# An attention and expert layer on one core: score chunks, rotation and maxima chunks in another order, and the first two sequences loaded, written and prepared by need

## The chip, the cores and the metric

One core of one Trainium2 chip runs the whole layer in one launch. The metric is the device time of that launch in microseconds, the median of several runs. The notes use these names: PE (TensorE), DVE (VectorE), ACT (ScalarE), POOL (GpSimd), SP (SyncE, which here only issues DMAs).

## What is computed

16 sequences of 256 tokens, width 128, go through causal attention with 16 heads of 8 and rotary position tables, a residual and a layer norm, then a layer of 8 experts of which each token takes one (its largest gate, with a capacity of 512 tokens an expert), a residual and a second layer norm.

```python
q = (x @ wq + bq); k = (x @ wk + bk); v = (x @ wv + bv)      # 16 heads of 8
q = _apply_rope(q, cos, sin); k = _apply_rope(k, cos, sin)
scores = jnp.einsum('bhqd,bhkd->bhqk', q, k) / jnp.sqrt(jnp.float32(HEAD_DIM)) + causal
attn = jax.nn.softmax(scores, axis=-1)
x = _layernorm(x + (attn @ v) @ wo + bo)
probs = softmax(x @ wg); idx = argmax(probs); mask = one_hot(idx)
locations = cumsum(mask) - mask; mask = mask * (locations < C)
x = _layernorm(x + gate * (W[idx] @ x + b[idx]))
```

## The kernel before

Every engine has its instruction stream written out by hand, with semaphores between them. The work is software-pipelined over the sequences. In step s the kernel works on sequence n = s + 2 (its transposes, its q and k projections, the rotation), a = s + 1 (its parts are written to DRAM and loaded back in another layout), b = s (row maxima of the scores, the v projection), c = s - 1 (scores again with the maximum subtracted, exp, product with v), d = s - 2 (division, output projection, first norm, gate, experts) and e = s - 3 (second norm, output). Steps run from -2 to 17. A step has 14 slots, and each engine's program lists what it does in slot 0, 1, 2 and so on. Within a slot the order is that of the code.

The scores of a sequence are cut into 11 chunks (`CHUNKS`): eight of two groups of heads, two of four, one of eight. In slot k + 2 PE makes chunk k of the scores of c in ps_b (line 820, "ps_b chunk"), ACT takes its exp (line 473), and in slot k + 3 PE multiplies it with v into ps_pv (line 853, "PV chunk k"). The maxima chunks are scores in ps_a (line 830), whose row maxima DVE takes (line 631). `maxima_at` places them: chunks 2 to 10 of b in slots 0 to 8, and chunks 0 and 1 of a in slots 12 and 13. ps_a and ps_b each have two banks, so chunk k waits for the reader of chunk k - 2.

```python
if slot < NCH - EARLY:
    return (b, slot + EARLY) if has(b) else (None, 0)
if slot >= SLOTS - EARLY:
    return (a, slot - (SLOTS - EARLY)) if has(a) else (None, 0)
```

When all row maxima of b are there, DVE widens them to heads and splits them into three bf16 parts in max_parts (lines 674 to 687), PE turns them (line 840, slot 11), ACT copies them to max_rows (line 495) and issues two DMAs that put them into q_plain (line 502), which the ps_b chunks of the next step read. After that ACT makes rot_1 (line 512) and then the exp of chunk 10.

The experts come in two blocks, one for each half of the tokens (`experts(d, n, 0)` in slot 12, `experts(d, n, 1)` in slot 13, lines 774 to 794). Both write ps_m, so the second waits until DVE has selected from the first (line 616). The gate (lines 692 to 709) and the capacity test (lines 713 to 725) are on DVE in slots 9 and 10, followed by the rotation's four products (lines 730, 733) and their addition (line 739). ACT splits off the first bf16 part (line 512) and POOL the other two (lines 424 to 430). SP writes the three parts in 12 DMAs (line 314), and once they have landed it loads k_plain and q_diag of a, the maxima operands (lines 326, 329), and then q_plain and k_diag of b, the operands of ps_b (lines 337, 340).

At the end of a step ACT copies the sums out of ps_pv (slot 13), and at the start of the next the weighted values (slot 0). DVE takes the reciprocals of the sums in slots 1 and 2 (line 640).

At the start SP loads the tables and weights, DVE clears v_diag, swaps and splits the weights, PE turns the biases (line 753), and only then come the first transposes (line 880) and projections (lines 774 to 776). In step -2 `start_late` prepares the expert weights (lines 560, 562, 764) and the bf16 tables (lines 566 to 570) behind the rotation of sequence 0. ACT writes the head marks into k_diag (`mark_heads`, line 448) in slot 6 of steps -1 and 0.

## Time and profile before

| | |
|---|---|
| median of 3 runs | 492.28 us (491.29 to 495.66) |
| the profiled execution's own time | 493.83 us |
| its span, first to last instruction | 492.2 us |
| mean granted TensorE clock | 0.948 |
| busy: PE, DVE, ACT, POOL | 418.6, 345.4, 169.0, 165.2 us |
| moved by DMA | 47.29 MB, mean 96 GB/s |

Busy time counts instructions from start to end. PE's matmuls overlap each other and their ends are modelled, so idle time in front of a matmul is shown a little short.

### The profile page before, as it was taken

What the parts mean: (1) busy time and instruction counts of PE and PEld (TensorE: products, weight loads), DVE (VectorE), ACT (ScalarE), POOL (GpSimd) and SP (SyncE); (2) the same over time, 40 slices, a digit from 0 to 9 for tenths busy, and PEclk for the clock granted to TensorE, in tenths of its full rate; (3) what the DMA queues carried; (4) which work ended last, traced back from release to release, by engine and by line L of the source; (5) the groups of instructions that cost most, each with busy time, mean ns of one, the idle gap of its engine ahead of it and who ended that gap; (6) DMA issues with size and microseconds to landing.
All of it is one profiled execution on the core that took longest, in us unless ns stands there. A gap on an engine that the chain in (4) does not pass through costs nothing.

```text
span 492.2 us, 10410 instructions
## 1 busy us (share of the span) xinstructions
PE 418.6 (85%) x3270; PEld 362.4 (74%) x3270; DVE 345.4 (70%) x910; ACT 169.0 (34%) x370; POOL 165.2 (34%) x288
## 2 busy tenths in 40 slices
PE   2527398999999999999999999999999999989551
PEld 2425287979788888888888878787879787868441
DVE  7677346678787877788787878778777786844542
ACT  4404134333342424243333434333434342424100
POOL 5423202131424242433424251525252523231232
PEclk9997588999999999999999999999999999999856
DMA  4163977939385856777585849393939393310000
GB/s 119 48 102 90 150 137 107 140 87 137 74 147 86 144 79 135 91 126 97 121 104 121 106 105 126 90 135 82 149 83 140 84 141 65 30 31 1 11 1 21
DMA packets 145443, 47.29 MB, mean 96 GB/s; under 512 B 104317, under 2 KB 141697, under 8 KB 145418
## 3 DMA queue, kind: packets, MB, share of 16 engines
q1 hardware_dynamic: 141194, 43.30, 55.0%
q10 hardware_dynamic: 3456, 1.57, 1.8%
q0 software_dynamic: 768, 2.10, 1.5%
q8 instruction: 13, 0.21, 0.2%
q14 instruction: 12, 0.10, 0.1%
HBM read 30.70 MB, written 14.68 MB: 92 GB/s over the span
## 4 chain that ended last, share of the span: by engine, by line
PE 65%; DVE 17%; issue 6%; ACT 5%; SPq 2%; DMA 2%; POOL 1%; ACTq 1%; DVEq 0%; POOLq 0%
PE ps_pv L853 27%; PE ps_m L774 6%; PE ps_b L820 5%; PE ps_m L775 5%; PE ps_m L776 5%; DVE y_sel L616 4%; PE ps_a L830 4%; PE ps_m L794 3%; PE ps_b L805 2%; ACT probs L473 2%; PE ps_a L805 2%; PE ps_n L861 2%; DMA k_diag<-plain_parts 1%; SPq L314 1%; PE ps_n L901 1%
## 5 line engine op out<-in xcount | busy, mean ns | idle before, releaser
L853 PE MATMUL ps_pv<-probs,v_diag 128*128 128x64 f32 (+3 forms) x1024 | 191.1, 322 | 6.1 <-ACT probs L473 6.1
L853 PEld LDWEIGHTS ps_pv<-probs,v_diag 128*128 128x128 f32 x1024 | 150.3, 193 | 16.1 <-ACT probs L473 9.1
L473 ACT ACTIVATE probs<-ps_b 128x512 f32<-128x512 f32 (+1 forms) x176 | 96.9, 559 | 141.3 <-PE ps_b L805 140.5
L631 DVE TENSOR_REDUCE row_max<-ps_a 128x2 f32<-128x512 f32 (+3 forms) x176 | 109.8, 634 | 36.7 <-PE ps_a L805 36.4
L830 PE MATMUL ps_a<-k_plain,q_diag 128*128 128x64 bf16 (+3 forms) x512 | 66.3, 242 | 12.9 <-DMA q_diag<-plain_parts 7.2
L820 PE MATMUL ps_b<-q_plain,k_diag 128*128 128x64 bf16 (+3 forms) x512 | 65.9, 237 | 2.1 <-DMA k_diag<-plain_parts 2.1
L616 DVE TENSOR_REDUCE y_sel<-ps_m 128x128 f32<-128x1024 f32 x32 | 39.2, 1225 | 38.0 <-PE ps_m L794 37.3
L830 PEld LDWEIGHTS ps_a<-k_plain,q_diag 128*128 128x128 bf16 x512 | 35.3, 102 | 23.4 <-DVE row_max L631 13.0
L820 PEld LDWEIGHTS ps_b<-q_plain,k_diag 128*128 128x128 bf16 x512 | 37.6, 99 | 10.2 <-DMA k_diag<-plain_parts 2.4
L413 POOL COPY v_diag<-v_rows 64x128 f32<-64x128 f32 x64 | 18.6, 291 | 78.2 <-ACT v_rows L487 76.2
L805 PE MATMUL ps_a<-mask_a_bf,ident_bf 128*128 128x128 bf16 (+2 forms) x176 | 44.6, 253 | 0.0
L424 POOL TENSOR_TENSOR rot_rest<-rot 128x512 f32<-128x512 f32 x16 | 18.6, 1159 | 76.7 <-ACT rot L512 63.0
L805 PE MATMUL ps_b<-mask_b_bf,ident_bf 128*128 128x128 bf16 (+2 forms) x176 | 43.4, 247 | 0.0
L350 POOL TENSOR_SCALAR rs<-mv 128x2 f32<-128x2 f32 x32 | 7.4, 230 | 100.6 <-DVE mv L601 100.6
L455 ACT ACTIVATE sums<-ps_pv 64x256 f32<-64x256 f32 x16 | 6.1, 381 | 83.0 <-PE ps_pv L853 83.0
L774 PE MATMUL ps_m<-we_hi,x1t_hi 128*128 128x512 f32 x64 | 29.7, 464 | 4.1 <-DVE y_sel L616 4.1
L640 DVE RECIPROCAL inv_den<-sums 128x128 f32<-128x128 f32 x32 | 29.8, 938 | 2.6 <-ACT sums L456 2.6
L774 PE MATMUL ps_m<-xt_hi,w_hi 128*128 128x256 f32 x64 | 21.2, 331 | 10.6 <-DVE xt_lo L669 10.6
L361 POOL TENSOR_SCALAR y_out<-z,mv,rs 128x128 f32<-128x128 f32 x32 | 25.5, 801 | 3.6 <-POOL rs L352 3.6
L775 PE MATMUL ps_m<-we_lo,x1t_hi 128*128 128x512 f32 x64 | 26.2, 410 | 0.0
L776 PE MATMUL ps_m<-we_hi,x1t_lo 128*128 128x512 f32 x64 | 26.1, 408 | 0.0
L794 PE MATMUL ps_m<-route_rows,route 128*128 128x512 f32 x64 | 26.0, 406 | 0.0
(141 smaller groups left out, 695.9 us busy)
## 6 DMA issues: line engine op xcount, KB each, us to landing
plain_parts<-rot SPq DMA_DIRECT2D x192, 64.0 KB, 2.0
k_plain<-plain_parts SPq DMA_DIRECT2D x16, 384.0 KB, 3.8
q_diag<-plain_parts SPq DMA_DIRECT2D x32, 192.0 KB, 5.4
q_plain<-plain_parts SPq DMA_DIRECT2D x16, 384.0 KB, 6.1
k_diag<-plain_parts SPq DMA_DIRECT2D x32, 192.0 KB, 6.5
x_in<-in_L_attn_x_dram SPq DMA_DIRECT2D x16, 128.0 KB, 5.7
x_res<-in_L_attn_x_dram SPq DMA_DIRECT2D x16, 128.0 KB, 3.1
out_dram<-y_out POOLq DMA_DIRECT2D x16, 128.0 KB, 2.5
```

The lines of the kernel that those rows point to most:

```text
L473: act.activation(probs[:, k % PR, 0:cols], ps_b[k % 2][:, 0:cols], ACT.Exp, scale=SCALE)\
L616: dve.tensor_reduce(y_sel[:, t, :], ps_m[:, :, :].rearrange("p a (e f) -> p f (a e)", e=4), AX.X, ALU.max).then_inc(s_["moe_taken"], 1)
L631: last = dve.tensor_reduce(row_max[:, NBLK - 1 - j, groups[0]:groups[-1] + 1], scores[:, :, col:col + width(j)], AX.X, ALU.max)
L640: dve.reciprocal(inv_den[:, half_cols], sums[:, half_cols]).then_inc(s_["den_done"], 1)
L774: pe.matmul(out, sh, mh, start=start, stop=False, skip_group_check=True)
L775: pe.matmul(out, sh, ml, start=False, stop=False, skip_group_check=True)
L776: return pe.matmul(out, sl, mh, start=False, stop=stop, skip_group_check=True)
L794: mm = pe.matmul(ps_m[:, h, :], route[:, tok], route_rows[:, 512 * h:512 * h + 512], start=False, stop=True, skip_group_check=True)
L805: return pe.matmul(v, ident_bf[:, :], rows, start=False, stop=True, skip_group_check=True)
L820: pe.matmul(ps_b[k % 2][:, col:col + width(j)], diag_block(k_diag[q], g, j), q_plain[q][:, g, BLK * j:S], start=(i == 0), stop=False, skip ...
L830: pe.matmul(ps_a[k % 2][:, col:col + width(j)], diag_block(q_diag[at], g, NBLK - 1 - j), k_plain[at][:, g, 0:width(j)], start=(i == 0), st ...
L853: mm = pe.matmul(ps_pv[:, g // 4, BLK * j:S], v_diag[q][:, j, 128 * g:128 * g + 128], probs[:, k % PR, col:col + width(j)], start=(j == 0 ...
```

## The change

1. Order on PE. Maxima chunks of b move to slots 0, 2, 3, 4, 5, 6, 7 and two in slot 8 (`MAXIMA_IN`). The turned maxima come behind the PV chunk of slot 11, and the second expert block behind the last PV chunk.
2. DVE. The second selection moves to slot 3 of the next step, the rotation's products ahead of the capacity test, and the first half of the reciprocals to slot 13 of the step before.
3. POOL takes over the widening and splitting of the maxima and the addition of the rotation. ACT copies sums and weighted values together in slot 13.
4. The start. Loads are split and ordered (identity, x, wq, bq, wk, bk, then wv and the rest, then the tables), each with its own semaphore. The turning of the biases moves behind the first transposes. `start_late` moves from step -2 to step -1. ACT makes the bf16 tables. For sequences 0 and 1, ACT issues the six writes of rot_1, and SP loads the ps_b operands directly behind the maxima operands.

```diff
+MAXIMA_IN = {0: (2,), 2: (3,), 3: (4,), 4: (5,), 5: (6,), 6: (7,), 7: (8,), 8: (9, 10)}
...
-            if slot < NCH - EARLY:
-                return (b, slot + EARLY) if has(b) else (None, 0)
             if slot >= SLOTS - EARLY:
-                return (a, slot - (SLOTS - EARLY)) if has(a) else (None, 0)
-            return None, 0
+                return [(a, slot - (SLOTS - EARLY))] if has(a) else []
+            return [(b, k) for k in MAXIMA_IN.get(slot, ())] if has(b) else []
...
-                    write(rot_1, 0, "rot1_done")
+                    if not (is_step(s, -1) or is_step(s, 0)):
+                        write(rot_1, 0, "rot1_done")
...
+                    if is_step(s, -1) or is_step(s, 0):
+                        sp.wait_ge(s_["start_pool"], 2 + 2 * a)
+                        load_b(a, q)
...
+                    after(pool, "a_taken", b, NCH, NCH)
+                    after(pool, "ex_ready", b)
+                    pool.tensor_tensor(max_wide[:, :, :].rearrange("p i (g h) -> p (i g) h", g=PAIRS),
...
+                    pool.tensor_copy(max_part(0), by_half(max_wide)).then_inc(s_["parted"], 1)
...
+                    after(pool, "roped", n, 1, 1)
+                    pool.tensor_tensor(rot[:, :, :], rot_c[:, :, :], rot_s[:, :, :], ALU.add).then_inc(s_["rot_done"], 1)
...
+            def write_part_1(n):
+
+                after(act, "rot1_done", n, 1, 1)
+                act.nop(nofuse=True)
+                for qk, taus in ((0, Q_PARTS[0]), (1, K_PARTS[0])):
+                    for tau in taus:
+                        act.dma_start(of_seq(plain, n)[qk, :, :, tau].rearrange("h d g x -> (h d) (g x)"),
+                                      rot_1[:, qk, :]).then_inc(s_["parts_written"], 16)
...
+                    if slot == 8 and is_step(s, -2):
+                        narrow_tables()
+                    if slot == 8 and is_step(s, -1):
+                        write_part_1(0)
+                        mark_heads(0)
+                    if slot == 12 and is_step(s, -1):
+                        write_part_1(1)
+                        mark_heads(1)
...
-                    if slot in (12, 13) and has(d):
-                        select(d, slot - 12)
-                    if slot in (1, 2) and has(d):
-                        after(dve, "sums_copied", d, 1, 1)
-                        half_cols = slice(128 * (slot - 1), 128 * slot)
-                        dve.reciprocal(inv_den[:, half_cols], sums[:, half_cols]).then_inc(s_["den_done"], 1)
+                    if slot == 12 and has(d):
+                        select(d, 0)
+                    if slot == 3 and has(e):
+                        select(e, 1)
+                    if slot == 13 and has(c):
+                        after(dve, "sums_copied", c, 1, 1)
+                        dve.reciprocal(inv_den[:, 0:128], sums[:, 0:128]).then_inc(s_["den_done"], 1)
+                    if slot == 0 and has(d):
+                        dve.reciprocal(inv_den[:, 128:S], sums[:, 128:S]).then_inc(s_["den_done"], 1)
...
-                    if slot == 10 and is_step(s, -2):
+                    if slot == 10 and is_step(s, -1):
                         start_late()
```

On PE, slots 11 to 13 of a step in the middle. ps_a and ps_b are the maxima and score chunks, ps_pv the PV chunks, `we_hi` with `x1t_hi` the experts. Before, from PV chunk 9 on:

```order
L853 MATMUL ps_pv<-probs,v_diag 128x128 [waits exp_done]
...
L830 MATMUL ps_a<-k_plain,q_diag 128x256 [waits a_taken]
...
L774 MATMUL ps_m<-we_hi,x1t_hi 128x512 [waits moe_taken]
...
L794 MATMUL ps_m<-route_rows,route 128x512
L853 MATMUL ps_pv<-probs,v_diag 128x64 [waits exp_done]
L853 MATMUL ps_pv<-probs,v_diag 128x64 x7
```

The changed kernel at the same place:

```order
L881 MATMUL ps_pv<-probs,v_diag 128x128 [waits exp_done]
...
L869 MATMUL ps_a<-k_plain,q_diag 128x256 [waits a_taken]
...
L881 MATMUL ps_pv<-probs,v_diag 128x64 [waits exp_done]
L881 MATMUL ps_pv<-probs,v_diag 128x64 x7
L814 MATMUL ps_m<-we_hi,x1t_hi 128x512 [waits moe_taken]
...
L834 MATMUL ps_m<-route_rows,route 128x512
```

The expert block that waits for the selection (`moe_taken`) has changed places with the last PV chunk.

On DVE, slots 9 to 13 of such a step. Before:

```order
L687 TENSOR_TENSOR max_parts<-max_rest,max_parts 128x4x2x8
L692 TENSOR_REDUCE logits<-ps_n 128x16
...
L719 SCALAR_TENSOR_TENSOR kept<-ps_n,chosen_f 128x16
...
L730 SCALAR_TENSOR_TENSOR rot_cs<-ps_m,bias_cols,cst 128x256
...
L739 TENSOR_TENSOR rot<-rot_cs 128x512
L631 TENSOR_REDUCE row_max<-ps_a 128x2
L616 TENSOR_REDUCE y_sel<-ps_m 128x128
L631 TENSOR_REDUCE row_max<-ps_a 128x2
L616 TENSOR_REDUCE y_sel<-ps_m 128x128
```

Now:

```order
L727 TENSOR_REDUCE logits<-ps_n 128x16 [waits logits_ready]
...
L753 SCALAR_TENSOR_TENSOR rot_cs<-ps_m,bias_cols,cst 128x256 [waits rot_done,qk_ready]
...
L768 SCALAR_TENSOR_TENSOR kept<-ps_n,chosen_f 128x16
...
L682 TENSOR_REDUCE row_max<-ps_a 128x2 [waits widened,a_ready]
L668 TENSOR_REDUCE y_sel<-ps_m 128x128 [waits moe_ready]
L682 TENSOR_REDUCE row_max<-ps_a 128x2 [waits a_ready]
L692 RECIPROCAL inv_den<-sums 128x128 [waits sums_copied]
```

The operations on the maxima and the addition are gone from DVE, the products stand ahead of the test `kept`, and a reciprocal stands where the second selection was.

On SP, the writes and loads of sequences 0 and 1 (the parts are plain_parts). Before:

```order
L314 DMA plain_parts<-rot 16x8x256 x12
L326 DMA k_plain<-plain_parts 96x2048
L329 DMA q_diag<-plain_parts 48x32x64 x2
L303 DMA x_in<-in_L_attn_x_dram 128x2x128
L314 DMA plain_parts<-rot 16x8x256 x12
L326 DMA k_plain<-plain_parts 96x2048
L329 DMA q_diag<-plain_parts 48x32x64 x2
L337 DMA q_plain<-plain_parts 96x2048
L340 DMA k_diag<-plain_parts 48x32x64 x2
```

Now, for sequence 0:

```order
L323 DMA plain_parts<-rot 16x8x256 [waits rot2_done]
L323 DMA plain_parts<-rot 16x8x256 x3
L323 DMA plain_parts<-rot 16x8x256 [waits rot3_done]
L323 DMA plain_parts<-rot 16x8x256
L336 DMA k_plain<-plain_parts 96x2048 [waits parts_written,start_pool]
L339 DMA q_diag<-plain_parts 48x32x64 x2
L302 DMA q_plain<-plain_parts 96x2048 [waits start_pool]
L305 DMA k_diag<-plain_parts 48x32x64 x2
```

Sequence 0's q_plain and k_diag stood behind all writes and maxima operands of sequence 1; now they follow their own maxima operands.

## Rows read from the trace of the kernel before

**Rows 1.** The page, part 1: busy time, share of the span, instructions.

```profile
PE 418.6 (85%) x3270; PEld 362.4 (74%) x3270; DVE 345.4 (70%) x910; ACT 169.0 (34%) x370; POOL 165.2 (34%) x288
```

**Rows 2.** ACT's timeline, one middle step: start, us, line, out<-in [idle before].

```profile
212.42 1.09 ACT L473 ACTIVATE probs<-ps_b 128x512 f32<-128x512 f32 x2
...
228.26 1.61 ACTq L502 DMA_DIRECT2D q_plain<-max_rows  x2
...
230.65 0.60 ACT L473 ACTIVATE probs<-ps_b 128x512 f32<-128x512 f32 x1
236.44 0.38 ACT L455 ACTIVATE sums<-ps_pv 64x256 f32<-64x256 f32 x1 [5.19 <-PE ps_pv L853]
...
238.03 0.60 ACT L473 ACTIVATE probs<-ps_b 128x512 f32<-128x512 f32 x1
```

**Rows 3.** PE's timeline in the same step: start, us, line, out<-in.

```profile
212.63 0.22 PE L805 MATMUL ps_a<-mask_a_bf,ident_bf 128*128 128x128 bf16 x1
213.07 1.13 PE L853 MATMUL ps_pv<-probs,v_diag 128*128 128x256 f32 x4 [0.22 <-ACT probs L473]
...
214.25 0.22 PE L805 MATMUL ps_b<-mask_b_bf,ident_bf 128*128 128x128 bf16 x1
214.31 0.33 PE L830 MATMUL ps_a<-k_plain,q_diag 128*128 128x192 bf16 x2
...
225.05 0.40 PE L820 MATMUL ps_b<-q_plain,k_diag 128*128 128x128 bf16 x4
...
227.24 0.22 PE L840 MATMUL ps_n<-stacked_bf,max_parts 128*128 128x64 bf16 x2 [0.40 <-DVE kept L719]
...
232.56 0.50 PE L774 MATMUL ps_m<-we_hi,x1t_hi 128*128 128x512 f32 x1 [0.15 <-DVE y_sel L616]
...
234.51 1.89 PE L853 MATMUL ps_pv<-probs,v_diag 128*128 128x64 f32 x16
...
237.47 0.34 PE L830 MATMUL ps_a<-k_plain,q_diag 128*128 128x192 bf16 x2 [0.24 <-DVE row_max L631]
```

**Rows 4.** Groups by line: busy us, mean ns of one | idle before it.

```profile
L616 DVE TENSOR_REDUCE y_sel<-ps_m 128x128 f32<-128x1024 f32 x32 | 39.2, 1225 | 38.0 <-PE ps_m L794 37.3
...
L424 POOL TENSOR_TENSOR rot_rest<-rot 128x512 f32<-128x512 f32 x16 | 18.6, 1159 | 76.7 <-ACT rot L512 63.0 <-issue 13.7
...
L739 DVE TENSOR_TENSOR rot<-rot_cs 128x512 f32<-128x512 f32 x16 | 11.1, 692 | 1.0
...
L687 DVE TENSOR_TENSOR max_parts<-max_rest,max_parts 128x64 bf16<-128x64 f32 x16 | 3.6, 225 | 0.6
```

**Rows 5.** DVE's timeline, the widening product in step 0 and in a middle step.

```profile
46.00 0.22 DVE L674 TENSOR_TENSOR max_wide<-row_max,cst 128x64 f32<-128x64 f32 x1
...
222.90 0.35 DVE L674 TENSOR_TENSOR max_wide<-row_max,cst 128x64 f32<-128x64 f32 x1
```

**Rows 6.** Timeline of the start, of SP, PE and DVE.

```profile
28.19 0.34 SPq L326 DMA_DIRECT2D k_plain<-plain_parts  x1
...
31.51 0.58 PE L774 MATMUL ps_m<-xt_hi,w_hi 128*128 128x256 f32 x1 [8.49 <-DVE xt_lo L669]
...
36.78 3.25 DVE L631 TENSOR_REDUCE row_max<-ps_a 128x2 f32<-128x512 f32 x5
...
37.61 8.01 SPq L314 DMA_DIRECT2D plain_parts<-rot  x12
...
54.52 0.61 PE L830 MATMUL ps_a<-k_plain,q_diag 128*128 128x256 bf16 x2 [6.62 <-DMA q_diag<-plain_parts]
...
59.40 0.61 PE L820 MATMUL ps_b<-q_plain,k_diag 128*128 128x256 bf16 x2 [2.07 <-DMA k_diag<-plain_parts]
```

**Rows 7.** The chain of waits, at the start and at the end: start, us, what.

```profile
8.60 2.30 PE ps_n L753 x10
...
47.12 0.33 SPq L326
...
459.54 1.74 PE ps_pv L853 x16
```

More of the change, by code:

```diff
@@ L474, in step @@
                             .then_inc(s_["exp_done"], 1)
-                    if slot == 0 and has(d):
-                        copy_pairs(weighted, 0).then_inc(s_["pv_copied"], 1)
                     if slot == 7 and has(d):
@@ L621, in step @@
                 for slot in range(SLOTS):
-                    t, k = maxima_at(slot, a, b)
-                    if t is not None:
+                    for t, k in maxima_at(slot, a, b):
                         after(dve, "a_ready", t, NCH, k + 1)
@@ L646, in step @@
                         dve.tensor_tensor(attn[:, :], weighted[:, :], inv_den[:, :], ALU.mult).then_inc(s_["normed"], 1)
-                    if slot == 3 and has(e):
+                    if slot == 4 and has(e):
                         add_experts(e)
@@ L710, in step @@
                                           ALU.is_equal).then_inc(s_["chosen_done"], 1)
+                    if slot == 9 and is_step(s, -2):
+                        split_wv()
+                    if slot == 10 and has(n):
+                        after(dve, "qk_ready", n, 1, 1)
+                        after(dve, "rot_done", n)
+                        for i in range(2):
+                            dve.scalar_tensor_tensor(out=rot_c[:, i, :], in0=ps_m[:, 0, S * i:S * i + S],
+                                                     scalar=bias_cols[:, 2 * i:2 * i + 1], in1=C("cos"),
+                                                     op0=ALU.add, op1=ALU.mult)
+                            last = dve.scalar_tensor_tensor(out=rot_s[:, i, :], in0=ps_m[:, 1, S * i:S * i + S],
+                                                            scalar=bias_cols[:, 2 * i + 1:2 * i + 2], in1=C("sin"),
+                                                            op0=ALU.add, op1=ALU.mult)
+                        last.then_inc(s_["roped"], 1)
                     if slot == 10 and has(d):
@@ L822, in step @@
                         masks(ps_b[k % 2], CHUNKS[k], mask_b_bf, False).then_inc(s_["b_ready"], 1)
-                    t, k = maxima_at(slot, a, b)
-                    if t is not None:
+                    for t, k in maxima_at(slot, a, b):
                         at = p if t is b else q
@@ L832, in step @@
                         masks(ps_a[k % 2], CHUNKS[k], mask_a_bf, True).then_inc(s_["a_ready"], 1)
-                    if slot == 13 and has(d):
-                        experts(d, n, 1)
-                    if slot == 11 and has(b):
-                        after(pe, "parted", b, 4, 4)
-                        if has(d):
-                            after(pe, "route_done", d, 1, 1)
-                        for i in range(NBLK // 2):
-                            mm = pe.matmul(ps_n[:, BLK * i:BLK * i + BLK],
-                                           max_parts[:, 2 * i:2 * i + 2, :].rearrange("p i m -> p (i m)"), stacked_bf[:, :],
-                                           start=(i == 0), stop=True, skip_group_check=True)
-                        mm.then_inc(s_["ex_ready"], 1)
                     if slot == 12 and has(d):
@@ L856, in step @@
                         mm.then_inc(s_["pv_ready"], 1)
+                    if slot == 11 and has(b):
+                        after(pe, "parted", b, 4, 4)
+                        if has(d):
+                            after(pe, "route_done", d, 1, 1)
+                        for i in range(NBLK // 2):
+                            mm = pe.matmul(ps_n[:, BLK * i:BLK * i + BLK],
+                                           max_parts[:, 2 * i:2 * i + 2, :].rearrange("p i m -> p (i m)"), stacked_bf[:, :],
+                                           start=(i == 0), stop=True, skip_group_check=True)
+                        mm.then_inc(s_["ex_ready"], 1)
+                    if slot == 13 and has(d):
+                        experts(d, n, 1)
                     if slot == 4 and has(d):
```

150 lines of the change are left out of this document (77 added, 73 removed).

## The prediction

> **What bounds the kernel now.** I read the page first, then the timelines of one middle step engine by engine, then the start and the chain of waits at the end. The reader is to see that TensorE is the bound: busy for 418.6 of 492.2 us [rows 1]. In the middle the steps repeat: exp 0 of a sequence starts at 212.42 and the next sequence's at 238.03, a step of 25.61 us [rows 2]. Of it PE stands still at four places [rows 3]: before PV chunk 0 (213.07, waits for exp 0), before a maxima chunk (237.47, waits for a row maximum), before the transposed maxima (227.24, wait for the capacity test on DVE) and before the second expert block (232.56, waits for the selection of the first). The idle shown is 0.22 + 0.24 + 0.40 + 0.15 = 1.01 us, but it counts only from the modelled end of the last matmul. A mask matmul that is followed at once has its successor 0.06 us after its own start (214.25, 214.31), and the one at 212.63 waits 0.44 us for its successor: issue really stopped for 0.38 us, 0.16 more than shown. So the four are 0.38 + 0.40 + 0.56 + 0.32 = 1.66 us, and 23.95 us of a step are work of PE. That is what the middle can give.
>
> The start is another matter: the first exp waits for PE's first ps_b matmul at 59.40, which waits for k_diag of sequence 0 [rows 6]. Those operands stand in SP's queue behind the writes and loads of sequence 1. The end is a serial chain of some 31 us after the last PV chunk, which ends at 461.3 [rows 7].
>
> **The start, edit by edit.** (a) The cover at the very beginning stays: DVE's memset of v_diag ends at 5.96 in either kernel and its swaps and splits run to about 10.5. The ten bias matmuls take 2.30 us from 8.60 [rows 7]; the transposes, xt_hi and xt_lo no longer stand behind them but ahead, so the projections of sequence 0 begin at 10.9, not 12.85: 1.95 us less. The rotation's addition goes to POOL: 1.16 us by the subtraction of the same shape there against 0.69 on DVE [rows 4]. rot_1 of sequence 0 is done at 17.4 (18.9 before).
> (b) Sequence 1's projections began at 31.51 [rows 6] behind the expert weights and DVE's narrowing copies. Now they need only xt_lo, after rot_1 on ACT: 18.3. ACT then issues six writes and marks the heads. At SP's pace (12 writes in 8.01 us, [rows 6]) six writes are 4.0 us, and the marking takes 4.2, so ACT is free at 26; POOL, with its memsets in between, ends the rotation's addition of sequence 1 at about 27.5. rot_1 of sequence 1 is done at 28.1, against 37.5.
> (c) SP issues only six writes for sequence 0, from POOL's rot_2 (19.4) on, to 23.5. The loads began 1.5 us after the last write's issue ended (45.62 to 47.12, [rows 6, 7]), so they begin at 25.2, not 28.19. Sequence 1's maxima operands were usable 7.4 us after the load's issue and sequence 0's k_diag behind them 12.3 us after it (47.12 to 54.52 and 59.40). Now both sets of sequence 0 go in a row: 32.6 and 37.5. The former wait of the first exp, k_diag, is gone by 22 us; what is late next?
> (d) The eleven row maxima of sequence 0 start at 33 instead of 36.78 [rows 6] and take 9 us as before, to 42. Then POOL splits them (2.4 us, below), PE turns them, ACT copies (0.6), issues two DMAs (2.3 there) and they land 2 us later: 49.7. Sequence 1: its writes queue behind the loads of sequence 0 (37.5), land at about 39.2, its loads are usable at 46.6, and three maxima chunks stand ahead of ps_b: 49.2. Both agree: ps_b at 49.7 instead of 59.40, the term is **-9.7 us**. If the three sets of loads slow each other it is -6; with no such delay and a shorter chain, -12.
>
> **The step in the middle.** Count from the end of PV chunk 10. (1) Four copies on ACT, 1.59 us (236.44 to 238.03, [rows 2]), then exp 0, 0.60. PE's cover was five chunks of scores; now it is the second expert block, 1.95 us (232.56 to 234.51, [rows 3]), and five groups of about 0.27: 3.3 us. exp 0 ends at 3.30. The stall of 0.38 shrinks to under 0.1. (2) The selection of the first block (1.23, [rows 4]) runs under PV 10 (1.74): 0.32 gone. (3) DVE loses the five widening operations (0.22 to 0.32 each, 1.5 us with gaps) and the addition (0.69), and the second selection sits behind row maximum 4, so maxima chunks find their buffers free within 0.1: 0.40 shrinks to 0.1. At the tight places, the pair of chunks in slot 8 and xt_lo, 0.1 to 0.4 us are in hand when the row maxima are laid out one behind another at 0.46 to 0.62 each. (4) The turned maxima stand behind PV 8 (0.99 us later), but the capacity test now stands behind the rotation products (1.65 us). From PV 0 (213.07), the projections are issued by 225.05 [rows 3] and done at +12.1, the products at +13.8, the test at +14.6; PE gets there at 227.24 - 0.56 + 0.99, +14.6. 0.56 shrinks to 0.1. (5) What is next: from the turned maxima ACT copies, issues DMAs for 1.61 us, copies rot_1, runs exp 10, which ends at 231.25, 4.0 us after 227.24 [rows 2, 3]. PE's work between is now also 4.0 us, because the expert block is behind PV 10: no slack, 0 to 0.1. (6) POOL's chain: last row maximum at 13.4 on this count, v_diag copies to 14.3, then five small operations. Such an operation has no row on POOL. Its ends are DVE's 0.22 for the same shape and POOL's 1.16 for 128x512 [rows 4]; I take 0.4, nearer the first, since it has an eighth of the columns, with gaps 2.1 in all: ready at 16.4, needed at 18.2. At the upper end 5.8 us would cost 1.9 a step, 27 in all. The addition on POOL ends some 2 us before ACT can take it, behind its DMA issues.
> Left over 0.15, so the step is **24.1 us, -1.5**. If the tight places add up, -0.9; if nothing is left, -1.66. SP's writes and loads start some 2 us later in a step, where the maxima operands have about 5 us in hand.
>
> A place where the trace and the notes speak against the change: the widening product on DVE took 0.22 us at 46.00 with POOL idle and 0.35 at 222.90 beside POOL's copies [rows 5]. The Trainium skill, SBUF — State Buffer, section "Who interferes with whom", says that a DVE instruction with two SBUF inputs and a GpSimd instruction that reads SBUF hold a shared port and the later one waits for the whole of the other. The trace agrees in kind, with 0.13 us. By that rule DVE's four router operations of this sort would each wait up to 0.4 us beside POOL's new chain, 1.6 us against 1.5 in hand: 0.1 a step, 1.4 in all.
>
> **The sum**, against the profiled execution (493.83 us; span 492.2 and 1.6 around it): start -9.7. The step with sequence 0's PV has no experts to cover ACT's chain, +0.8. The next -1.3, since the row maxima bound its start less. Eleven steps at -1.5: -16.5. Two steps near the end, with 2.2 us of stalls each, -1.9 each: -3.8. The last PV step: PV 0 waited 1.7 and the selection 0.6, and its second expert block (1.95) now runs behind the last PV chunk (459.54 to 461.3) under the copies and reciprocals; the late selection delays z1, which waits for nothing else there, by 0.55: -3.7. Together -34.2: 459.6. The median of the runs is 1.55 below the profiled execution, so I predict 458.
>
> **Rivals.** A: the stalls of the middle only change place (maxima pair, exp 10): -0.3 a step. Speaks for it that three places have under 0.15 us in hand; against it that DVE has 2.2 us less to do in a step. Then 16 us less gain: 474. B: the start gives only 3 us, since sequence 0's second set and sequence 1's first came together once before, between 47.12 and 59.40 [rows 6, 7], and now more of them lie close, and ACT's issues delay rot_1. Against it that most loads now start earlier, one after another. Then 465. C, slower: POOL's five small operations. If each took 1.5 us (7.5 with no gap, against the 4.0 us between 14.3 and 18.3), the turned maxima would come 3.5 us late in each of 14 steps, +49 over the sum: 507. It decides from 1.3 us an operation, where 2.4 us a step eats all the gain. For it: nothing but that the shapes are split in halves and POOL has no row for them. Against it: 1.16 us for eight times the columns. D: the addition on POOL holds rot_1 on ACT and so exp 10 (the change does not do what it says): it would have to be over 2 us later than I have it; at 1 us beyond, +14: 472.
>
> **How the numbers follow.** Forecast (start -6 to -12, step -1.2 to -1.66) 0.70; A 0.10; B 0.12; C 0.02; D 0.04; 0.02 for no change by several of them. The forecast's own ends are 452 and 466. To hold 8 in 10, B and part of A have to be in: 451 to 470. A change of 1% (5 us) is about what a measurement of this kernel can tell from none. Only C and the remainder reach that: faster 0.96, same 0.02, slower 0.02.
>
> **What would show it.** First ps_b matmul at about 50 us, ended by the maxima rows' DMA or by q_diag of sequence 1, not k_diag. exp 0 to exp 0 24.1 us. PE idle in a middle step under 0.3 us shown, with nothing before the second expert block. POOL's five small operations under 0.5 us each and done before PE asks. The second expert block of the last step behind the last PV chunk. I am wrong if the first ps_b is after 54, if a step is above 24.8, or if PE waits for max_parts or for exp 10 by more than 0.3 us in each step.

## The result, and the profile after

The changed kernel takes **461.94 us** (median of 4 runs, 461.80 to 464.61) against 491.78 us for the kernel before in the same comparison (4 runs, 489.36 to 495.66). The ratio is 0.940, 95% interval 0.933 to 0.947. Predicted were 458.0 us and a range of 451 to 470.

The page of the profiled execution (461.80 us, span 460.1), parts 1 and 2; the second part is in 40 slices of the span:

```profile
PE 410.3 (89%) x3270; PEld 359.2 (78%) x3270; DVE 317.8 (69%) x809; ACT 170.4 (37%) x375; POOL 207.8 (45%) x384
...
PE   3548598999999999999999999999999999999651
...
PEclk9999798999999999999999999999999999999957
```

PE is still the bound, with the same 3270 matmuls. DVE has 101 instructions fewer and POOL 96 more [rows 1].

The steps. ACT's timeline, the first exp of a sequence each time: the very first; sequences 2 and 13, which enclose eleven steps in the middle; and the two ends of the middle step that is read below:

```profile
53.81 0.60 ACT L517 ACTIVATE probs<-ps_b 128x512 f32<-128x512 f32 x1 [3.20 <-PE ps_b L845]
...
102.86 0.60 ACT L517 ACTIVATE probs<-ps_b 128x512 f32<-128x512 f32 x1 [1.01 <-PE ps_b L845]
...
199.82 0.60 ACT L517 ACTIVATE probs<-ps_b 128x512 f32<-128x512 f32 x1 [0.99 <-PE ps_b L845]
...
224.12 1.15 ACT L517 ACTIVATE probs<-ps_b 128x512 f32<-128x512 f32 x2 [0.99 <-PE ps_b L845]
...
369.28 0.60 ACT L517 ACTIVATE probs<-ps_b 128x512 f32<-128x512 f32 x1 [0.91 <-PE ps_b L845]
```

(369.28 - 102.86) / 11 = 24.22 us a step, where the kernel before has 25.61 [rows 2]. The stalls are gone. PE's timeline of that step, in order: turned maxima, last PV chunk, second expert block, the maxima chunk of slot 0 and the first PV chunk of the next sequence. All but the last PV chunk are the places of [rows 3]:

```profile
215.48 0.22 PE L890 MATMUL ps_n<-stacked_bf,max_parts 128*128 128x64 bf16 x2
...
219.53 2.00 PE L881 MATMUL ps_pv<-probs,v_diag 128*128 128x64 f32 x16
221.34 0.48 PE L814 MATMUL ps_m<-we_hi,x1t_hi 128*128 128x512 f32 x1
...
224.51 0.34 PE L869 MATMUL ps_a<-k_plain,q_diag 128*128 128x192 bf16 x2
...
224.77 1.13 PE L881 MATMUL ps_pv<-probs,v_diag 128*128 128x256 f32 x4
```

None of these lines shows an idle time (in brackets, it would be the wait in front of the instruction). Over the step, PE's idle time adds up to 0.11 us against 1.01. POOL's timeline of the same step shows its new chain, and DVE's the one place where it costs something:

```profile
211.75 0.29 POOL L424 TENSOR_TENSOR max_wide<-row_max,cst 128x64 f32<-128x64 f32 x1 [0.25 <-POOL v_diag L419]
212.18 0.24 POOL L431 CAST max_parts<-max_wide 128x64 bf16<-128x64 f32 x1
212.50 0.31 POOL L433 TENSOR_TENSOR max_rest<-max_wide,max_parts 128x64 f32<-128x64 f32 x1
212.94 0.24 POOL L437 CAST max_parts<-max_rest 128x64 bf16<-128x64 f32 x1
213.26 0.30 POOL L439 TENSOR_TENSOR max_parts<-max_rest,max_parts 128x64 bf16<-128x64 f32 x1
...
214.90 1.28 POOL L448 TENSOR_TENSOR rot<-rot_cs 128x512 f32<-128x512 f32 x1 [0.16 <-POOL seen L444]
```

```profile
215.57 0.63 DVE L774 TENSOR_TENSOR gate_kept<-n_kept,gate 128x2 f32<-128x2 f32 x1
```

The five operations end at 213.56, 1.9 us before PE asks.

The start is where the time fell short. PE's timeline there, the waits alone, then ACT's:

```profile
32.21 0.58 PE L869 MATMUL ps_a<-k_plain,q_diag 128*128 128x256 bf16 x2 [4.44 <-DMA q_diag<-plain_parts]
...
43.91 0.58 PE L814 MATMUL ps_m<-xt_hi,w_hi 128*128 128x256 f32 x1 [1.11 <-DVE xt_lo L722]
...
46.65 0.33 PE L890 MATMUL ps_n<-stacked_bf,max_parts 128*128 128x64 bf16 x2
...
53.08 0.59 PE L860 MATMUL ps_b<-q_plain,k_diag 128*128 128x256 bf16 x2 [3.43 <-DMA q_plain<-max_rows]
```

```profile
47.60 2.28 ACTq L550 DMA_DIRECT2D q_plain<-max_rows  x2
```

The first exp starts 6.3 us earlier than before (53.81; it was at 60.15), and what it waits for is no longer k_diag [rows 6] but the two DMAs of max_rows, whose issue ended at 49.88 and which landed at 53.08. (A landing is read here from the start of the first ps_b matmul that waited for it.)

By spans, 492.2 to 460.1: start -6.3, the step of the first PV +0.7 (24.14), the next -1.4 (24.91), eleven steps -15.4, the two behind them -4.4 (22.48 and 21.67), from the last exp 0 to the end -5.2 (46.67). Together -32.1; predicted were -34.2.

### The profile page after: what moved, and what is told of

The parts are those of the page before. It is cut to its first block and busy times, and to the rows that moved or that the text cites. A ratio compares the mean times of both kernels' runs of the same rounds, so it can differ in the third digit from the quotient of the medians.

```text
span 460.1 us, 10441 instructions
## 1 busy us (share of the span) xinstructions
PE 410.3 (89%) x3270; PEld 359.2 (78%) x3270; DVE 317.8 (69%) x809; ACT 170.4 (37%) x375; POOL 207.8 (45%) x384
## 5 line engine op out<-in xcount | busy, mean ns | idle before, releaser
L881 PEld LDWEIGHTS ps_pv<-probs,v_diag 128*128 128x128 f32 x1024 | 148.0, 192 | 12.0 <-ACT probs L517 6.2
L682 DVE TENSOR_REDUCE row_max<-ps_a 128x2 f32<-128x512 f32 (+3 forms) x176 | 108.3, 631 | 22.3 <-PE ps_a L845 21.9
L419 POOL COPY v_diag<-v_rows 64x128 f32<-64x128 f32 x64 | 18.4, 288 | 68.6 <-PE ps_pv L881 33.9
L860 PEld LDWEIGHTS ps_b<-q_plain,k_diag 128*128 128x128 bf16 x512 | 36.3, 98 | 11.5 <-issue 4.2
L692 DVE RECIPROCAL inv_den<-sums 128x128 f32<-128x128 f32 x16 | 15.2, 953 | 37.0 <-ACT sums L483 37.0
L814 PE MATMUL ps_m<-we_hi,x1t_hi 128*128 128x512 f32 x64 | 28.6, 448 | 1.3 <-DVE y_sel L668 1.3
L753 DVE SCALAR_TENSOR_TENSOR rot_cs<-ps_m,bias_cols,cst 128x256 f32<-128x256 f32 x32 | 15.3, 479 | 19.5 <-PE ps_m L816 19.5
L448 POOL TENSOR_TENSOR rot<-rot_cs 128x512 f32<-128x512 f32 x16 | 20.6, 1288 | 14.2 <-DVE rot_cs L756 12.5
```

The costliest lines, as they stand in the source:

```text
L682: last = dve.tensor_reduce(row_max[:, NBLK - 1 - j, groups[0]:groups[-1] + 1], scores[:, :, col:col + width(j)], AX.X, ALU.max)
L814: pe.matmul(out, sh, mh, start=start, stop=False, skip_group_check=True)
L860: pe.matmul(ps_b[k % 2][:, col:col + width(j)], diag_block(k_diag[q], g, j), q_plain[q][:, g, BLK * j:S], start=(i == 0), stop=False, skip ...
L881: mm = pe.matmul(ps_pv[:, g // 4, BLK * j:S], v_diag[q][:, j, 128 * g:128 * g + 128], probs[:, k % PR, col:col + width(j)], start=(j == 0 ...
```

## The experiments

Each is an edit of the changed kernel. A step is the mean of the same eleven as above; in the changed kernel and the six runs that alter only its start it is 24.20 to 24.23, so a tenth of a microsecond there is a difference. Where no interval is given, the time is that of one execution. The first exp comes at 53.4 to 55.5 us in the changed kernel and the six runs that alter its middle, so 1 us there tells nothing by itself.

**start_alone**: all orders of PE and DVE, POOL's share and ACT's copies as in the kernel before; the start as changed.

```diff
-MAXIMA_IN = {0: (2,), 2: (3,), 3: (4,), 4: (5,), 5: (6,), 6: (7,), 7: (8,), 8: (9, 10)}
+MAXIMA_IN = {i: (i + 2,) for i in range(9)}
...
-                    if slot == 12 and has(d):
-                        experts(d, n, 0)
+                    if slot in (12, 13) and has(d):
+                        experts(d, n, slot - 12)
...
```

> The changed kernel with its whole middle undone (orders on PE and DVE, POOL's share, ACT's copies), so only the start of the change is left. Theory T (start and middle are independent, the middle's gain is made of stalls of PE in each step): first exp at 53.8 us as in the changed kernel, a step in the middle back at 25.6, last exp 0 to the end 51.9, about 486 us, ratio 0.987. Rival R (part of the middle's gain comes from the later transfers and loads of the start, or the start's gain is given back in the first full steps): time outside 483 to 489, or a step away from 25.6 by over 0.2 us.

Measured: ratio 0.984 (0.9805 to 0.9876), median 482.66 us; the profiled execution, its longest, 487.16. First exp at 54.10, step (384.90 - 102.84) / 11 = 25.64, PE's idle in a middle step the same 1.01 us at the same four places as [rows 3], last exp 0 to the end 52.0. By the step, the first exp and the end, T holds: start and middle are independent. The median lies 0.3 us below the 483 at which R's range begins, the profiled execution fits T's 486. The start is worth 1.6% of the kernel, the middle and end the other 4.4.

Next, one part of the middle undone at a time.

**dve_splits**: widening, splitting and addition back on DVE, in slots 9 and 10.

```diff
-                    after(pool, "a_taken", b, NCH, NCH)
...
-                    pool.tensor_tensor(rot[:, :, :], rot_c[:, :, :], rot_s[:, :, :], ALU.add).then_inc(s_["rot_done"], 1)
...
+                        after(dve, "a_taken", b, NCH, NCH)
...
+                        dve.tensor_tensor(rot[:, :, :], rot_c[:, :, :], rot_s[:, :, :], ALU.add).then_inc(s_["rot_done"], 1)
```

> The changed kernel with widening and splitting of the maxima and the addition of the rotation back on DVE, all orders as changed. Theory T (DVE has room: some 22 of 24.2 us busy; the orders on PE removed the stalls, and POOL's part only took DVE's work off): the step stays within 24.2 to 24.6, total 462 to 467. Rival P (the offload is what buys the middle, since DVE's row maxima would again be late): the step goes to 25.0 or more, with PE idle before maxima chunks or before the turned maxima by over 0.6 us a step, total over 472.

**expert_ahead**: second expert block ahead of the last PV chunk, second selection in slot 13.

```diff
-                    if slot == 12 and has(d):
-                        select(d, 0)
-                    if slot == 3 and has(e):
-                        select(e, 1)
+                    if slot in (12, 13) and has(d):
+                        select(d, slot - 12)
...
-                    if slot == 12 and has(d):
-                        experts(d, n, 0)
+                    if slot in (12, 13) and has(d):
+                        experts(d, n, slot - 12)
...
```

> The changed kernel with the second expert block back ahead of the last PV chunk and the second selection back in slot 13. Theory T (stalls of their own places): the waits before the second expert block (0.3) and before PV chunk 0 (0.4) come back, the step is 24.8 to 24.9, and the tail from the last exp 0 grows by about 2 us: total about 472. Rival A (the stalls only change place): the step stays below 24.4.

**maxima_even**: the maxima chunks one to a slot.

```diff
-MAXIMA_IN = {0: (2,), 2: (3,), 3: (4,), 4: (5,), 5: (6,), 6: (7,), 7: (8,), 8: (9, 10)}
+MAXIMA_IN = {i: (i + 2,) for i in range(9)}
```

> The changed kernel with the maxima chunks one to a slot again, chunks 2 to 10 in slots 0 to 8. Theory T: the wait before the maxima chunk of slot 0 or 1 comes back in part (0.1 to 0.4 us a step): step 24.3 to 24.6, total 463 to 468. Rival N (the places of the maxima chunks do not matter now that DVE is relieved): step 24.2 within 0.05, total within 1 us of 462.

**test_ahead**: on DVE the block of the capacity test stands ahead of the block of the rotation's products, both in slot 10.

```diff
+                    if slot == 10 and has(d):
+                        after(dve, "egate_done", d, 1, 1)
...
                     if slot == 10 and has(n):
...
-                    if slot == 10 and has(d):
-                        after(dve, "egate_done", d, 1, 1)
...
```

> The changed kernel with the capacity test on DVE ahead of the rotation's products again. Theory T (each edit keeps DVE's queue just in time for PE; the products may be a little later, since rot_1 waited for ACT and not for POOL in the changed kernel, 1.85 us): step 24.2 to 24.5, the wait before the turned maxima (0.07) gone, total 462 to 466. Rival D (POOL's addition then comes too late for rot_1 and exp 10, or DVE stands behind the location matmuls): step 24.8 or more, with PE waiting before PV chunk 10, ps_b chunk 10 or the next experts.

**turned_ahead**: the turned maxima ahead of the PV chunk of slot 11.

```diff
+                    if slot == 11 and has(b):
+                        after(pe, "parted", b, 4, 4)
...
                     k = slot - PV_SLOT
...
-                    if slot == 11 and has(b):
-                        after(pe, "parted", b, 4, 4)
```

> The changed kernel with the turned maxima ahead of PV chunk 8 again. Theory T (the capacity test on DVE ends just when PE arrives, 0.07 us late, so whatever PE does before it is cover): PE waits some 1.0 us there in every step, step 25.1 to 25.3, total 474 to 478. Rival A (the stall is made good by the slack that exp 10 gains): PE waits, but the step stays below 24.6.

| | time, us | step, us | over the changed kernel's 24.22 |
|---|---|---|---|
| dve_splits | 478.39 | 25.30 | +1.08 |
| expert_ahead | 485.20 | 25.57 | +1.35 |
| maxima_even | 476.05 | 25.27 | +1.05 |
| test_ahead | 468.24 | 24.72 | +0.50 |
| turned_ahead | 471.76 | 25.11 | +0.89 |
| the whole middle (start_alone) | 482.66 | 25.64 | +1.42 |

Undone alone, the five cost 4.87 us a step; the whole middle undone costs 1.42. (start_alone also puts back the reciprocals, ACT's copy of the weighted values and the addition of the experts' output, which no run undoes alone.) PE's timelines of one middle step each say where. dve_splits:

```profile
248.08 0.22 PE L892 MATMUL ps_n<-stacked_bf,max_parts 128*128 128x64 bf16 x2 [1.11 <-DVE kept L770]
```

expert_ahead, the maxima chunk of slot 0 and the second expert block:

```profile
233.37 0.34 PE L866 MATMUL ps_a<-k_plain,q_diag 128*128 128x192 bf16 x2 [1.30 <-DVE row_max L682]
...
252.65 0.49 PE L811 MATMUL ps_m<-we_hi,x1t_hi 128*128 128x512 f32 x1 [0.15 <-DVE y_sel L668]
```

maxima_even, the chunks of slots 0 and 1:

```profile
231.03 0.34 PE L869 MATMUL ps_a<-k_plain,q_diag 128*128 128x192 bf16 x2 [0.24 <-DVE row_max L682]
...
232.43 0.34 PE L869 MATMUL ps_a<-k_plain,q_diag 128*128 128x192 bf16 x2 [0.74 <-DVE row_max L682]
```

test_ahead, the first expert block, and turned_ahead, the turned maxima:

```profile
220.63 0.49 PE L814 MATMUL ps_m<-we_hi,x1t_hi 128*128 128x512 f32 x1 [0.64 <-DVE rot_cs L771]
```

```profile
218.50 0.22 PE L879 MATMUL ps_n<-stacked_bf,max_parts 128*128 128x64 bf16 x2 [0.97 <-DVE kept L768]
```

Every one of these waits ends with DVE, although it is far from full: 19.65 of 25.27 us busy in dve_splits, 18.86 of 25.53 in expert_ahead. What counts is not its busy share but what stands in its queue in front of the instruction that PE waits for. DVE's timeline in expert_ahead, just before PE's wait, shows how:

```profile
231.82 0.95 DVE L690 RECIPROCAL inv_den<-sums 128x128 f32<-128x128 f32 x1 [1.31 <-ACT sums L483]
232.69 0.63 DVE L682 TENSOR_REDUCE row_max<-ps_a 128x2 f32<-128x512 f32 x1
```

The reciprocal of slot 13 waits 1.31 us for ACT's copy of the sums and takes 0.95, and the row maximum for which PE waits stands behind it. In the changed kernel PE spends those microseconds in the second expert block. In the kernel before this wait was absent too, because the reciprocals stood in slots 1 and 2. So the early reciprocal needs the late expert block, and the free slot 1 of `MAXIMA_IN` is room for the second reciprocal, which maxima_even fills. This is read from DVE's timeline; no run undoes such a pair together. By the expectations: P holds for dve_splits, and T is wrong. For expert_ahead A is wrong (the stall comes back) and so is T, by a factor of two (25.57, not 24.9). For maxima_even both are wrong, since 25.27 is 0.7 above the top of T's range. For test_ahead, 24.72 lies between T's 24.5 and D's 24.8; the wait is one of those that D names: the expert block needs ps_m, which the rotation's products read. turned_ahead came as T said (25.11 a step), with a total 2 us under T's range.

Then the start.

**start_by_sp**: sequences 0 and 1 written by SP alone, their ps_b operands loaded in their own steps.

```diff
-                    if not (is_step(s, -1) or is_step(s, 0)):
-                        write(rot_1, 0, "rot1_done")
+                    write(rot_1, 0, "rot1_done")
...
-                    if is_step(s, -1) or is_step(s, 0):
-                        sp.wait_ge(s_["start_pool"], 2 + 2 * a)
-                        load_b(a, q)
-                if has(b) and not (is_step(s, 0) or is_step(s, 1)):
+                if has(b):
+                    if is_step(s, 0) or is_step(s, 1):
+                        sp.wait_ge(s_["start_pool"], 2 + 2 * b)
...
-                        write_part_1(0)
...
-                        write_part_1(1)
```

> The changed kernel, but sequences 0 and 1 written by SP alone (no writes from ACT) and their ps_b operands loaded in their own steps, behind the next sequence's writes and loads, as before. Everything else of the start stays as changed. Theory L (the order of writes and loads is the larger part of the start's 6.3 us): first exp at 57 to 59, since k_diag of sequence 0 again stands behind sequence 1's set. Rival C (compute order is what brought the gain: projections of sequence 1 at 18.4 instead of 31.5): first exp below 55.5, and SP's transfers early enough anyway.

Measured 462.04 us, first exp at 52.96: not later than in the changed kernel. L is wrong, C holds. Once the projections come early, k_diag of sequence 0 is there in time in the old order too, and no gain of writes and loads "by need" shows. (The total hides 1.5 us: the end takes 48.21 us here, for which see the last steps below.)

**late_early**: `start_late` of DVE and PE in step -2 again.

```diff
-                    if slot == 10 and is_step(s, -1):
+                    if slot == 10 and is_step(s, -2):
                         start_late()
...
```

> The changed kernel with the expert weights' preparation (DVE and PE) back in step -2, ahead of sequence 1's transposes. Theory L: sequence 1 is written some 10 us later, but the chain of sequence 0 does not need it, so the first ps_b moves only by what the third maxima chunk of sequence 1 adds: first exp at 55 to 58. Rival C: the first exp goes back by over 5 us, to 59 or more.

Measured 466.12 us, first exp at 58.34, 4.5 us later: between the two expectations, and outside the scatter. PE's timeline:

```profile
30.13 0.58 PE L814 MATMUL ps_m<-xt_hi,w_hi 128*128 128x256 f32 x1 [8.93 <-DVE xt_lo L722]
...
57.61 0.59 PE L860 MATMUL ps_b<-q_plain,k_diag 128*128 128x256 bf16 x2 [3.36 <-DMA q_plain<-max_rows]
```

Neither sequence 1's chunks (the third at 53.54) nor its own data hold ps_b, but again max_rows: issued until 52.47, landed 5.1 us later, behind sequence 1's loads, which SP issued from 45.26 to 50.82.

**b1_in_step_1** and **short_chain** ask whether that landing depends on the bytes in flight or on when the chain ends. The first, timed again as b1_repeated:

```diff
-                    if is_step(s, -1) or is_step(s, 0):
+                    if is_step(s, -1):
                         sp.wait_ge(s_["start_pool"], 2 + 2 * a)
                         load_b(a, q)
-                if has(b) and not (is_step(s, 0) or is_step(s, 1)):
+                if has(b) and not is_step(s, 0):
+                    if is_step(s, 1):
+                        sp.wait_ge(s_["start_pool"], 2 + 2 * b)
```

> The changed kernel, only sequence 1's q_plain and k_diag are loaded in step 1 and not behind its maxima operands. Theory Q (the two DMAs of max_rows landed 3.2 us after their issue and not 2.0, because these 0.75 MB were moving): they land within 2.2 us, the first exp is 1 us earlier, at 52.8. Rival K (the landing time is that of the DMAs themselves, or another set takes that place): within 0.3 us of 53.8.

short_chain, where besides the lines shown DVE widens and splits for sequence 0, behind its last row maximum:

```diff
-                    if slot == 11 and has(b):
+                    if slot == (9 if is_step(s, 0) else 11) and has(b):
                         after(pe, "parted", b, 4, 4)
```

> The changed kernel, for sequence 0 alone: DVE widens and splits the maxima (some 1.0 us instead of POOL's 1.8), and PE turns them ahead of the projections of sequence 2, not behind them (46.65). Theory E (the chain row maxima, split, turn, ACT, DMA sets the first exp): turned at 44.5, first exp at 51.7 to 52.3, total 1.5 to 2.1 us less than 461.9. Rival S (sequence 1's operands and its third maxima chunk, at 49.2, are as late): first exp above 53.3.

The repetition of the first:

> The kernel of b1_in_step_1 again, timed in rounds, since one execution gave 456.77 us. Theory Q: the gain over the changed kernel (461.9) is 4 to 5 us and holds over executions: median 456 to 458, ratio 0.925 to 0.935. Rival V (that execution was one of the short ones): median 460 or more, ratio 0.935 to 0.94.

b1_in_step_1 took 456.77 us, first exp 51.18; the repetition 458.92 (457.80 to 459.78, 6 runs), ratio 0.932 (0.928 to 0.937), first exp 52.17. short_chain took 460.98, first exp 53.80. The waits of ps_b and the issue of max_rows, in b1_repeated:

```profile
47.62 2.28 ACTq L552 DMA_DIRECT2D q_plain<-max_rows  x2
```

```profile
51.45 0.58 PE L862 MATMUL ps_b<-q_plain,k_diag 128*128 128x256 bf16 x2 [1.78 <-DMA q_plain<-max_rows]
```

and in short_chain:

```profile
45.02 2.28 ACTq L551 DMA_DIRECT2D q_plain<-max_rows  x2
```

```profile
53.07 0.59 PE L881 MATMUL ps_b<-q_plain,k_diag 128*128 128x256 bf16 x2 [2.35 <-DMA q_plain<-max_rows]
```

b1_repeated against the changed kernel is the clean pair: with sequence 1's 0.75 MB out of the way, the DMAs issued at the same moment (47.62 and 47.60) land 1.6 us after their issue's end, not 3.2. (The 128 KB load of x_in, which stands behind them in SP's queue, went out 2.8 us earlier with it.) short_chain is less clean. Its DMAs were issued 2.6 us earlier and landed at 53.07 instead of 53.08, but SP's loads of sequence 1 also went out 1.4 us later, first the changed kernel's, then its own:

```profile
40.25 0.33 SPq L336 DMA_DIRECT2D k_plain<-plain_parts  x1
```

```profile
41.70 0.32 SPq L336 DMA_DIRECT2D k_plain<-plain_parts  x1
```

So the landing moved with the loads; what the earlier issue alone would have gained stays open. Q holds for b1_in_step_1 and E is wrong. S has the time right but not the cause: ps_b waited for max_rows. K is wrong on the time, but right that another set stands close behind. In b1_in_step_1 the turned maxima came 1.7 us earlier than in the changed kernel, and ps_b then started directly behind sequence 1's third maxima chunk, with no wait for max_rows:

```profile
49.89 0.61 PE L871 MATMUL ps_a<-k_plain,q_diag 128*128 128x256 bf16 x2 [0.25 <-DVE row_max L684]
...
50.40 0.64 PE L862 MATMUL ps_b<-q_plain,k_diag 128*128 128x256 bf16 x2
```

The windows view of the DMA engines and PE's clock (us, PE busy, PEclk, DMA share, GB/s), first the changed kernel, then b1_repeated. The share adds up packets that overlap and can pass 1:

```profile
48.00:52.00 4.00, 0.56 (x5) 0.88 1.46 133
52.00:56.00 4.00, 2.92 (x14) 0.50 0.43 108
56.00:60.00 4.00, 4.00 (x23) 0.76 0.34 87
```

```profile
48.00:50.00 2.00, 0.45 (x3) 1.00 0.13 25
...
52.00:54.00 2.00, 2.00 (x13) 0.50 0.41 105
54.00:56.00 2.00, 2.00 (x14) 0.96 0.42 108
```

Of the 3 us between the medians, 1.6 are the first exp. The next step is 1.3 us shorter (22.84, not 24.14): PE had stood still for 1.78 us and not 3.43, and was back at its upper clock by about 54 us and not 58. On b1_repeated against the rival V: its ratio is as Q has it, its median 0.9 us above Q's 458.

**start_in_turn**: all of it together; SP's loads as in start_by_sp, ACT's writes kept, short_chain's edit, and the expert rows prepared in step 1.

```diff
+                    if slot == 11 and is_step(s, 1):
+                        start_rows()
```

> The changed kernel with another start: SP loads the ps_b operands of sequences 0 and 1 in their own steps again (behind the next sequence's maxima operands) while ACT keeps the six writes of rot_1 for both; for sequence 0 DVE widens and splits the maxima and PE turns them ahead of the projections; the expert rows are prepared on DVE in step 1 and not before the first row maxima. Theory Q (the start is bound by the bytes queued ahead of max_rows and, behind that, by the chain of row maxima and TensorE's half clock after a standstill): max_rows issued by 46, landed by 48.5, first exp at 48.3 to 50, next step 22.4, total 452 to 456, ratio 0.92 to 0.93. Rival K (sequence 1's maxima operands and its three chunks take the place): first exp at 51 or later, total 456 to 458.

Measured: five executions of 457.94 to 460.88 us, median 459.77, and a sixth of 1399.01 that is left out; ratio 0.934 (0.929 to 0.940); max_rows issued from 45.20, first exp at 51.35. The first exp is rival K's, and so is the cause: ps_b follows directly behind sequence 1's third maxima chunk (at 49.90). The total is above both expectations. The start gained 2.5 us, and the next two steps (23.53 and 25.81) gave back 0.3: PE turned the maxima ahead of sequence 2's projections, and that sequence's writes began at 51.40, not at 50.68 as in the changed kernel; its maxima operands and, behind them, sequence 1's ps_b operands came late:

```profile
68.19 0.39 PE L893 MATMUL ps_a<-k_plain,q_diag 128*128 128x256 bf16 x2 [1.34 <-DMA q_diag<-plain_parts]
...
74.15 0.58 PE L884 MATMUL ps_b<-q_plain,k_diag 128*128 128x256 bf16 x2 [1.81 <-DMA k_diag<-plain_parts]
```

The end took 48.34 us, 1.7 more than in the changed kernel (the last steps below say why). The best version found is therefore the small one, b1_in_step_1: its seven executions (456.8 to 459.8) all lie below the changed kernel's four (461.8 to 464.6), though they were not measured side by side and the intervals of the two ratios overlap.

## Why the prediction was right, and where it was wrong

**The start, -9.7: mis-sized, measured -6.3.** Steps (a) and (b) held: projections of sequence 0 at 10.80 (10.9), of sequence 1 at 18.37 (18.3), the addition on POOL 1.30 us (1.16), the maxima operands usable at 32.2 (32.6). That k_diag would no longer be waited for held. The idea behind (c), that the new order of loads is what removes it, fell with start_by_sp: the early projections do it without. late_early shows 4.5 of the 6.3 us in the place of `start_late`, which lets sequence 1's projections come early; no run takes the rest apart. The failed step is (d). Row maxima ended at 43.5, not 42 (+1.5: DVE was in `start_late` until 33.9, and PE worked on sequence 2's transposes in between). POOL took 2.0, not 2.4 (-0.4). PE turned them at 46.65, because sequence 2's projections, which waited for DVE's xt_lo, stood ahead in its queue (+1.2, not seen at all). The landing took 3.2 us, not 2.0 (+1.2): no row stood behind the 2 us, and I did not ask what the change had put in flight at that moment. Rival B named this collision (loads now lie close) but put it on the operands. The four make up the 3.4 us that were missing, but for rounding. Shown as a cause is the landing: b1_repeated takes the bytes away and gets 1.6 us back. What the other three cost by themselves stays open; short_chain, which took the second and third away, gained nothing, with its loads 1.4 us later. A second estimate, sequence 1's operands with three chunks at 49.2, came out at nearly the same time. That was no confirmation: ps_b did not wait for them here. It did in b1_in_step_1 and start_in_turn, at 50.40 and 50.41, so this limit lies close behind.

The third of the four has PE's clock in it. The twelve matmuls of sequence 2's projections took 2.74 us up to the turned maxima here and 1.63 in b1_in_step_1. One of them, here and there:

```profile
44.72 0.41 PE L814 MATMUL ps_m<-xt_hi,w_hi 128*128 128x256 f32 x1
```

```profile
43.81 0.28 PE L816 MATMUL ps_m<-xt_hi,w_hi 128*128 128x256 f32 x1
```

They start 0.21 us apart here and 0.11 there, a factor of two, though the granted clock of that stretch is recorded as 1.00 in both. b1_repeated, the same kernel as b1_in_step_1, has the slow pace; its first exp is 1.0 us later.

Two figures of the working do not agree with the rest of it. (d) takes 2.4 us for POOL where (6) arrives at 2.1. The forecast's lower end is 453.5 and not 452, since -12 at the start and -1.66 a step take 2.3 and 2.2 us off 458. Nothing rests on either. And the total came closer than its parts: the start and the first thirteen steps together fell 4.3 us short of the forecast, and the last two steps and the end brought 2.2 more, of which 1.4 by luck.

**The step, -1.5: -1.40, right.** All four stalls are gone as (1) to (4) said: 0.22, 0.24, 0.40 and 0.15 us shown [rows 3], together 0.11 now. (5) held: PV chunk 10 follows 0.04 us late, with no slack. (6) held: POOL's five operations took 0.24 to 0.31 us each (0.4 taken), ready with 1.9 us in hand (1.8). Rivals A, C and D are out. But the account behind the total was wrong in one respect: it gave each stall to one edit, as if they added up. The single undoings show that they do not add up: leaving out any one of the five costs 0.5 to 1.35 us a step, 4.87 in all, where the working reckoned with 1.66 for all stalls together. Had one of them been missing from the change, the time would have been 468 to 485 us, and this working would have shown a few us of it.

**Last steps -3.8 and -3.7: measured -4.4 and -5.2.** The wait for attn behind the last PV chunk shrank from 3.21 to 1.30 us; the next, for x1, grew from 3.16 to 3.92 by the late selection (0.55 predicted). The rest was not foreseen, and 1.4 of it was luck. PE's timeline, the last expert block, before and then after, whose eight matmuls are spread over 3.15 and 1.72 us from first start to last start:

```profile
478.34 0.79 PE L774 MATMUL ps_m<-we_hi,x1t_hi 128*128 128x512 f32 x1 [1.32 <-DVE y_sel L616]
```

```profile
447.70 0.50 PE L814 MATMUL ps_m<-we_hi,x1t_hi 128*128 128x512 f32 x1 [1.31 <-DVE y_sel L668]
```

The granted clock there was 0.56 before and 1.00 after, which is 1.4 us. That the change did not bring this is shown by start_by_sp and start_in_turn, whose last steps are the same program: their last eight matmuls were spread over 3.15 us again (clock 0.65 and 0.50), and from the last exp 0 to the end they took 48.21 and 48.34 us instead of 46.67.

**DVE beside POOL.** The Trainium skill, SBUF — State Buffer, section "Who interferes with whom": by the rule that DVE's operation with two SBUF inputs and POOL's read lock each other out for a whole instruction, four router operations were to wait beside POOL's five. In this step one operation of the router took 0.28 us, not 0.18, beside POOL's copy of v_diag, and none was held up by the five. The trace agrees with the rule at a place that was not forecast: gate_kept (0.63 us at 215.57; 0.16 in the kernel before) ends at 216.20, POOL's addition (from 214.90, 1.28) at 216.18. Over the sixteen steps gate_kept takes 0.64 in the median. PE shows no wait behind it, so the 0.1 us a step priced for the rule was not paid.

## What to carry to other kernels

In a hand-written pipeline that is nearly full, stalls are not a list to be added up: several edits can depend on one another, so price the set by the work of the bound engine (23.95 us here, 24.22 reached), and ask of any single edit what it costs when its partners are missing. Look at what stands in front of the awaited instruction in its own engine's queue before at how busy that engine is. For a small transfer on the critical path, ask which large ones are in flight when it is issued: here putting 0.75 MB off by one step let the small one land 1.6 us sooner for the same moment of issue, and the kernel took 3 us less.

## What the hardware showed

- The same two DMAs (48 KB each, 2.28 us to issue on ACT) landed 1.6 us after their issue with the DMA engines at 0.13 share, and 3.2, 5.1 and 5.8 us after it when SP's loads had been issued shortly before, although they are on another queue (q10, not q1). The Trainium skill, DMA: Bandwidth & Descriptors, section "Queues, rings and completion order", says that an engine takes turns between its queues, and that the increment of a semaphore lands only after every earlier write of that engine, in whatever queue. Both would make a small transfer late beside large ones. The landings here agree with that and do not separate the two: the issue that was 2.6 us earlier (short_chain) landed at 53.07 instead of 53.08, but its large loads had gone out 1.4 us later.
- The standstill before the first ps_b cost more than itself: after 3.43 us of it PE made the first chunks at the granted clock of 0.50 (1.2 GHz) until about 58 us, and after 1.78 us in b1_repeated until about 54. The step there was 1.3 us shorter.
- The recorded clock of the start is not enough by itself: in the changed kernel matmuls of 256 columns started 0.21 us apart at 44 to 46 us, and in b1_in_step_1 0.11 apart, with 1.00 recorded for both.
- POOL does the 128x64 operations in 0.24 to 0.31 us, DVE in 0.20 to 0.23 (in dve_splits); at 128x512 it is 1.28 against 0.69.
